# A third batch's front taken early: batch 2's first transposes, logits and projections run beside the first searches, every queue gets a new order, and the bias matmul contracts over 96 rows

## The chip, the core and the metric

One core of one Trainium2 chip runs the whole program. The metric is the device time of one execution in microseconds (us), here the median of three executions. TensorE is called PE (its weight loads PEld), VectorE DVE, ScalarE ACT, GpSimd POOL and SyncE SP. PE's clock is granted at one of two levels, 1.2 or 2.4 GHz; a profile writes them as 0.5 and 1.00.

## The reference, cut to what matters

```
x: (4, 512, 256)                       # 4 batches of 512 tokens, 16 row tiles of 128 tokens
xn = layernorm(x)
# layer 0, attention-like: cumulative sum over tokens
q, k, v = xn Wq + bq, xn Wk + bk, xn Wv + bv
context = (elu(q)+1) * cumsum((elu(k)+1) * v) / 4
# layer 0, genes
logits = (rms(xn) * norm_w) Wc^T / temperature        # (tokens, 512)
w = softmax(top 32 of 512 logits)                     # the "search": 4 rounds of 8 maxima
e = w @ genes[top];  ffn = tanh(e Wd^T) * rms(xn) * norm_w * (e Wu^T) * scale
x = x + context Wo^T + bo + ffn
xn = layernorm(x)
# layer 1: r = rms(xn); q,k,v = r w_qkv; gated cumulative sums -> y;
#   u, g = y w_swiglu;  out += (u * silu(g)) w_out
# layer 1: 16 experts, 2 per token, + a shared expert (352 hidden) on every token
```

## The kernel before, in words

All five engines get one long list of calls, written out by hand or by a planner; each call (a closure of `build`) waits on semaphores, issues its instructions and increments a semaphore. Nothing is reordered: an engine that waits in one call holds all calls behind it. So the order of the five lists is the schedule.

A batch b goes through a *front* (layer 0), a *middle* (layer 1's gated sums), and *shared chunks*; after all batches come the *expert tiles*.

- Front. DVE `stats1(b)` and `ratio1(b)` and ACT `lroot1(b)` make the layer norm's numbers, ACT `normal(b, i)` (L618) applies them to row tile i, PE `turn1(b, h)` (L299) transposes, ACT `xcopy1` (L622) copies out of PSUM into FE. PE `logits(b, i)` makes 128x512 logits in a PSUM bank, PE `kproj`, `vproj`, `qproj` (each with j = 0, 1) the projections, also in banks (all of these through `products`, L280). The operands are f32, and the profile shows each such product as two matmul records. DVE searches: `topa`, `topb`, `tope`, `topf`, `topg` (L954 to L978) per row tile; ACT `expert`, `unsel`, `total`, `emcopy` and POOL `topc` turn the result into weights; PE `emturn` (L328) and `express` apply them to the genes; PE `ffn` (L344, with 96 rows) and `oproj(b, j)` follow. `oproj` first writes the bias (L351: `w_one` times `bo_r`, 64 rows: a rounded part, a rest and zeros, in f32r), then eight matmul records of Wo on top (L355). DVE `joined` (L1001) ends the front.
- Middle. `stats2`, `lroot2`, `normal2`, `xroot`, PE `turn2`, `turnr`, `qproj2`, `kproj2`, `vproj2`, `meanq` (L395), `meank` (L400), `gates`; the operands are split in a rounded and a rest part (f32r), three matmuls for one product. DVE `qhat` (L1011), `khat` (L1018), `wsum`, `divisor`, `refine` and POOL `qfold`, `kfold`, `correct`, `quotient` belong to it.
- Shared chunks: for k = 0 to 10, PE `dgate(b, k)`, `dup(b, k)`, `ddown(b, k)` with ACT `dact`, `dround` and DVE `dtanh`, `dtimes` between them. They depend only on their own batch, and are strewn through the PE list as filler. Two buffers (HS, HQ) hold a chunk, so chunk k + 2 may begin when `ddown` of k is done.
- Expert tiles: 47, each PE `xturn(j)`, `xup(j)`, `hturn(j)`, `xdown(j)`, with two or three buffers for each step, and POOL fetching rows (`xfetch`) and scattering them (`yput`). The address of a tile's weights comes from registers that `locate` fills.

Banks 0 to 5 rotate; each call names its bank, and `take` waits for the last reader of it. Batch b uses the buffers FA to FG of b % 2, so batch 2's front can start only when batch 0 has left them: FA[0] is refilled by `fetch(2)` after `yspill(0)`, and FB to FE pass from batch 0's middle.

Where the PE list had nothing to do beside the first searches, `awake(n)` issues 2n matmul records on a constant tile `still` (L292); the list has 35 of them, 10 ahead of the first transpose, 15 up to the express of batch 0, 10 around the first `turn2`.

Weights that are split in two f32r parts come in pieces: SP `stagein(n)` loads piece n, ACT `prep(n)` (L587) makes the rounded part, POOL `prep(n)` (L1293) the rest. `PREP` lists them; `HIDDEN` and `DOWN` say how many must be ready for chunk k (nine for the gate and up products of k = 9 and 10, ten for ddown from k = 7 on). All nine are loaded in the first microseconds.

Of the kernel before, what the change touches and what calls it, by code (L numbers as in the profile page):

```python
# [8 lines left out]
F32R = mybir.dt.float32r  # L9
# [5 lines left out]
P = 128  # L15
# [15 lines left out]

TILES = 47
# [20 lines left out]
    "yh yl xh xl dg tg g2 du dh r0 rl rlp dw od "  # L53

# [29 lines left out]
def build(nc, x, vec, cst, wqkv0, wo0, wc, genes, wdu, wqkv1, wsg, wout, gate, sgu, sdn, gu, dn, part_d, out):  # L84
    with ExitStack() as ctx:
# [31 lines left out]
        w_one, bo_r = tile("w_one", P, F32R, 64), tile("bo_r", D, F32R, 64)  # L117
# [79 lines left out]
        d_xb, d_yb = sem("d_xb"), sem("d_yb")  # L197
# [3 lines left out]
        d_stage = [sem(f"d_stage{n}") for n in range(3)]  # L201
# [1371 lines left out]
```

## Time and profile before

| | us |
|---|---|
| median of 3 executions | 531.91 (530.75 to 852.44) |
| span of the profiled execution, first to last instruction | 529.7 |
| what the median has beyond that span | 2.2 |

The profiled execution has no time of its own beside its span; 531.91 - 529.7 = 2.2 us is taken as what lies around it. PE is busy in 507.5 us, DVE in 354.0, ACT in 296.0 and POOL in 272.7. "Busy" is the union of the records; a matmul record ends by a model about 0.17 us after its successor has begun, so the rate of PE is read from start to start.

### The profile page before, as it was taken

What the parts mean: (1) busy time and instruction counts of PE and PEld (TensorE: products, weight loads), DVE (VectorE), ACT (ScalarE), POOL (GpSimd) and SP (SyncE); (2) the same over time, 40 slices, a digit from 0 to 9 for tenths busy, and PEclk for the clock granted to TensorE, in tenths of its full rate; (3) what the DMA queues carried; (4) which work ended last, traced back from release to release, by engine and by line L of the source; (5) the groups of instructions that cost most, each with busy time, mean ns of one, the idle gap of its engine ahead of it and who ended that gap; (6) DMA issues with size and microseconds to landing.
All of it is one profiled execution on the core that took longest, in us unless ns stands there. A gap on an engine that the chain in (4) does not pass through costs nothing.

```text
span 529.7 us, 7444 instructions
## 1 busy us (share of the span) xinstructions
PE 507.5 (96%) x2488; PEld 384.8 (73%) x2488; DVE 354.0 (67%) x735; ACT 296.0 (56%) x577; POOL 272.7 (51%) x207
## 2 busy tenths in 40 slices
PE   7989999988999999999997999999999999999995
PEld 5565577766577766877885888887777777777684
DVE  4999995786998998847899895743232323323347
ACT  3788798785767758767653636225343343424321
POOL 0475648383472373383256346464576576666510
PEclk9999999998999999999999999999999999999999
DMA  8900031026020001037001850583322232223267
GB/s 271 372 6 1 1 124 37 0 100 220 1 80 40 1 1 41 1 129 243 1 1 44 292 179 14 187 232 98 108 91 89 71 100 83 97 80 89 71 242 265
DMA packets 19813, 54.32 MB, mean 103 GB/s; under 512 B 3312, under 2 KB 5792, under 8 KB 19776
## 3 DMA queue, kind: packets, MB, share of 16 engines
q1 hardware_dynamic: 15264, 41.52, 22.7%
q0 software_dynamic: 4512, 12.33, 7.7%
q8 instruction: 21, 0.34, 0.3%
q14 instruction: 16, 0.13, 0.1%
HBM read 36.14 MB, written 17.74 MB: 102 GB/s over the span
## 4 chain that ended last, share of the span: by engine, by line
PE 74%; DVE 15%; DMA 4%; issue 3%; ACT 2%; POOL 1%; SPq 1%; DVEq 0%; POOLq 0%; ACTq 0%
PE bank L280 52%; PE bank L442 9%; PE bank L355 3%; PE bank L474 2%; PE bank L501 2%; DMA fa<-in_x 2%; DMA ga<-y_rows 2%; DVE tk L972 1%; DVE m L970 1%; PE bank L328 1%; DVE fe L1029 1%; PE bank L400 1%; PE bank L292 1%; DVE tk L978 1%; DVE rw L1235 1%
## 5 line engine op out<-in xcount | busy, mean ns | idle before, releaser
L1214 DVE TENSOR_TENSOR m_h<-m_h,bank 128x176 f32<-128x176 f32 x47 | 15.8, 337 | 82.9 <-ACT m_h L789 82.9
L280 PE MATMUL bank<-mw,m_xt 128*128 x188 | 66.4, 476 | 0.2
L1362 POOL DMA_INDIRECT y_rows<-m_y,dest x47 | 46.9, 997 | 30.7 <-DVE m_y L1221 20.9
L1356 POOL DMA_INDIRECT xg<-xn_rows,tab x47 | 45.5, 969 | 28.0 <-PE bank L474 19.3
L280 PE MATMUL bank<-yhr,wsg_h 128*128 128x512 f32 x128 | 56.0, 437 | 0.8 <-ACT fc L721 0.8
L280 PE MATMUL bank<-hyr,wsg_h 128*128 128x512 f32 x128 | 50.1, 392 | 0.0
L280 PE MATMUL bank<-yhr,wsg_l 128*128 128x512 f32 x128 | 50.1, 391 | 0.0
L280 PE MATMUL bank<-mw,m_ht 88*128 x188 | 48.3, 379 | 0.0
L280 PE MATMUL bank<-fe,w_qkv 128*128 128x512 f32 x96 | 44.5, 594 | 0.6 <-ACT fe L622 0.6
L1347 POOL TENSOR_TENSOR hs0r<-hs,hq0r 128x512 fp32r<-128x512 f32 (+1 forms) x17 | 23.4, 1374 | 39.8 <-ACT hq0r L776 39.8
L280 PEld LDWEIGHTS bank<-mw,m_ht 88*128 88x128 f32 x188 | 35.2, 189 | 11.1 <-issue 0.4
L280 PEld LDWEIGHTS bank<-mw,m_xt 128*128 128x128 f32 x188 | 32.0, 189 | 14.9 <-issue 2.3
L789 ACT ACTIVATE m_h<-bank 128x176 f32<-128x176 f32 x47 | 14.9, 317 | 46.5 <-PE bank L280 46.5
L1098 DVE SCALAR_TENSOR_TENSOR hs<-hs,bank 128x512 f32<-128x512 f32 (+1 forms) x44 | 29.9, 680 | 14.7 <-PE bank L280 7.9
L1301 POOL TENSOR_TENSOR tk<-tk 128x512 f32<-128x512 f32 x16 | 21.3, 1334 | 27.9 <-ACT tk L680 27.8
L1347 POOL TENSOR_TENSOR hs1r<-hs,hq1r 128x512 fp32r<-128x512 f32 (+1 forms) x16 | 21.1, 1321 | 28.0 <-ACT hq1r L776 28.0
L782 ACT ACTIVATE m_xt<-bank 128x256 f32<-128x256 f32 x47 | 17.9, 381 | 29.9 <-PE bank L474 29.9
L572 ACT ACT_TABLE_LOAD x23 | 29.5, 1283 | 6.7 <-PE bank L442 5.6
L1088 DVE SCALAR_TENSOR_TENSOR hs<-hs,bank 128x512 f32<-128x512 f32 (+1 forms) x33 | 22.4, 680 | 15.4 <-ACT hs L771 15.4
L280 PEld LDWEIGHTS bank<-fe,w_qkv 128*128 128x128 f32 x96 | 17.5, 190 | 18.2 <-issue 16.3
L280 PE MATMUL bank<-w_wc,fe 128*128 128x512 f32 x64 | 29.9, 594 | 0.9 <-DVE w_wc L859 0.9
L280 PEld LDWEIGHTS bank<-yhr,wsg_h 128*128 128x128 f32 x128 | 24.1, 189 | 7.5 <-issue 1.7
(241 smaller groups left out, 1419.7 us busy)
## 6 DMA issues: line engine op xcount, KB each, us to landing
mw<-in_gu SPq DMA_DIRECT2D x16, 352.0 KB
ga<-y_rows SPq DMA_DIRECT2D x8, 512.0 KB, 8.1
mw<-in_dn SPq DMA_DIRECT2D x16, 176.0 KB
wsg_w<-in_wsg SPq DMA_DIRECT2D x4, 512.0 KB, 14.8
spilled_r<-fb SPq DMA_DIRECT2D x4, 512.0 KB, 2.8
spilled_x<-fa SPq DMA_DIRECT2D x4, 512.0 KB, 4.0
xn_rows<-fg SPq DMA_DIRECT2D x4, 512.0 KB, 3.6
hx<-spilled_x SPq DMA_DIRECT2D x4, 512.0 KB, 3.7
```

The costliest lines, as they stand in the source:

```text
L280: mm = e.matmul(o, a, b, start=n == 0, stop=n == len(terms) - 1)
L355: mm = e.matmul(o[:, i * D:(i + 1) * D], FF[b % 2][:, c, t:t + P], wov[:, c, :], start=False, stop=i + c == 2, skip_group_check=True)
L442: mm = e.matmul(o, a, w[0:m, r, :], start=k == 0 and i % 2 == 0 and z == 0, stop=False, skip_group_check=True)
L572: e.preload_act_table_set(name)
L782: e.activation(m_xt[j % 2][:, :], ps("jx", j)[:, 0:D], ACT.Copy).then_inc(s["jxc"], 1)
L1088: e.scalar_tensor_tensor(h, h, 1.0, ps("dg", b, k)[0:m, :], ALU.add, ALU.mult).then_inc(s["g2"], 1)
L1098: e.scalar_tensor_tensor(h[0:m, 1, :], h[0:m, 0, :], 1.0 if DIRECT[b] else 0.5, ps("du", b, k)[0:m, :], ALU.mult, ALU.mult).then_inc(s["dh ...
L1214: e.tensor_tensor(m_h[j % 3][:, :], m_h[j % 3][:, :], ps("ju", j)[:, 176:352], ALU.mult).then_inc(s["jh"], 1)
L1301: e.tensor_tensor(em, em, w, ALU.subtract).then_inc(s["tc"], 1)
L1347: e.tensor_tensor(HSr[c % 2][0:m, 0, :], HS[c % 2][0:m, 1, :], HQ[c % 2][0:m, 0, :].bitcast(F32), ALU.subtract).then_inc(s["rlp"], 1)
L1356: e.indirect_dma_start(out=xg[j % 3][:, :], out_offset=None, in_=xn_d, in_offset=bass.IndirectOffsetOnAxis(ap=tab[:, j:j + 1], axis=0)).th ...
L1362: e.indirect_dma_start(out=y_d, out_offset=bass.IndirectOffsetOnAxis(ap=dest[:, j:j + 1], axis=0), in_=m_y[j % 3][:, :], in_offset=None).t ...
```

## The change

Batch `EARLY` = 2 gets buffers of its own for the part of its front that has no search in it:

```diff
+        EA = also("early_x", stage_at, 1024)...          # its x, normalised x, transposed x:
+        ED = also("early_n", stage_at + 1024, 1024)...   # where HX, XH, HY are later
+        EE = big(also("early_t", stage_at + 2048, 1024))
+        EL = [also(f"early_l{n}", wsg_at + 4096 * n + 3072, 1024)... for n in range(2)]   # logits
+        EQ = {"q": big(also("early_q", stage_at + 8 * 1024, 1024)), "k": big(also("early_k", wout_at + 1024, 1024)), "v": ...}
```

New calls: SP `efetch` loads x[2] into EA (`fetch(2)` into FA[0] stays, for the residual sum). ACT `enormal(0..3)` writes ED, PE `eturn(0..1)` transposes it, ACT `excopy(0..1)` writes EE. PE `elogits(0..3)` and `eproject(0..5)` do for batch 2 what `logits(2, i)` and `kproj`, `vproj`, `qproj(2, j)` did, and ACT `elcopy(0..3)` and `epcopy(0..5)` carry the ten results from PSUM to EL and EQ:

```diff
+            def elogits(i, n):
+                q.wait_ge(s["wcf"], 2)
+                o = take(("el", i), n, s["ec"], i + 3)
+                q.wait_ge(s["ec"], i // 2 + 1)
+                products(o[:, :], [(EE[:, c, i * P:(i + 1) * P], wcv[:, c, :]) for c in range(2)]).then_inc(s["eg"], 1)
+            def elcopy(i):
+                q.wait_ge(s["eg"], i + 3)
+                e.activation(EL[i // 2][:, i % 2, :], ps("el", i)[:, :], ACT.Copy).then_inc(s["ec"], 1)
```

`topa(2, i)`, `expert(2, i)`, `phi(2, ...)` and `vtimes(2, j)` read EL and EQ in place of banks; `turn1(2)`, `xcopy1(2)`, `logits(2)` and the six projections of batch 2 are gone; `normal(2, i)` stays (FD is a factor of the ffn's product) and waits for `fetch(2)`. `stats1(2)` and `lroot1(2)` read EA and have small tiles of their own.

EL and EQ lie where the pieces 8 and 9 of the split weights go, so these are loaded late:

```diff
+                if n == 8:
+                    q.wait_ge(s["em"], 4 * EARLY + 4)
+                if n == 9:
+                    q.wait_ge(s["pv"], 2 * EARLY + 2)
-                e.dma_start(w[:, o:o + k], ap[:, o:o + k]).then_inc(d_stage[(n - 1) // 3], 16)
+                e.dma_start(w[:, o:o + k], ap[:, o:o + k]).then_inc(d_stage[STAGED[n]], 16)
...
+                else:                                    # xback(0); yback(0) waits for ec >= 12
+                    q.wait_ge(s["exn"], 4)
+                    q.wait_ge(s["eg"], 2)
```

The bias has 96 rows (64 before; the third block of 32 is zeros):

```diff
-        w_one, bo_r = tile("w_one", P, F32R, 64), tile("bo_r", D, F32R, 64)
+        w_one, bo_r = tile("w_one", P, F32R, 96), tile("bo_r", D, F32R, 96)
-    bo[0::32] = a["L0_attn_bo"]
+    bo[0:64:32] = a["L0_attn_bo"]
```

All five lists are new. Of the 35 `awake` the first 10 stay. The first third of the PE list, before and after:

```diff
-            awake(10); turn1(0, 0, 0); logits(0, 0, 1); turn1(0, 1, 2); logits(0, 1, 3); logits(0, 2, 4); kproj(0, 0, 5); kproj(0, 1, 0); vproj(0, 0, 2)
-            logits(0, 3, 1); vproj(0, 1, 5); turn1(1, 0, 0); awake(2); emturn(0, 0, 3); awake(2); express(0, 0, 3); qproj(0, 0, 4); awake(5); emturn(0, 1, 0); logits(1, 0, 1)
-            express(0, 1); emturn(0, 2, 0); awake(4); emturn(0, 3, 0); express(0, 2); awake(2); turn1(1, 1, 0); express(0, 3); logits(1, 1, 2); qproj(0, 1, 5)
-            kproj(1, 0, 1); kproj(1, 1, 0); ffn(0, 0, 4); vproj(1, 0, 5); ffn(0, 1, 3); ffn(0, 2, 1); logits(1, 2, 2); ffn(0, 3, 4); oproj(0, 0, 3)
...
+            awake(10); turn1(0, 0, 0); logits(0, 0, 1); turn1(0, 1, 0); logits(0, 1, 2); kproj(0, 0, 0); kproj(0, 1, 3); turn1(1, 0, 1)
+            logits(0, 2, 4); logits(0, 3, 1); qproj(0, 0, 0); emturn(0, 0, 3); vproj(0, 0, 2); vproj(0, 1, 3); express(0, 0, 5); eturn(0, 2)
+            eturn(1, 3); emturn(0, 1, 2); logits(1, 0, 3); express(0, 1); elogits(0, 4); elogits(1, 1); elogits(2, 4); elogits(3, 2)
+            logits(1, 1, 4); emturn(0, 2, 2); qproj(0, 1, 1); emturn(0, 3, 2); turn1(1, 1, 0); express(0, 2); express(0, 3); eproject(2, 0)
+            eproject(3, 2); eproject(4, 5); ffn(0, 0, 3); ffn(0, 1, 1); ffn(0, 2, 4); logits(1, 2, 0); ffn(0, 3, 5); kproj(1, 0, 2); kproj(1, 1, 3)
+            oproj(0, 0, 5); oproj(0, 1, 2); eproject(5, 4); vproj(1, 0, 3); vproj(1, 1, 0); logits(1, 3, 2); emturn(1, 0, 0); eproject(0, 3)
+            eproject(1, 5); turnr(0, 0, 4); turn2(0, 0, 1); turn2(0, 1, 0); express(1, 0, 3); emturn(1, 1, 5); turnr(0, 1, 1); qproj(1, 0, 0)
...
```

In the other lists: DVE makes `stats1(2)` and `ratio1(2)` between the searches of row tiles 1 and 2 of batch 0, and `topa(2, 0)`, `(2, 1)`, `(2, 2)`, `topb(2, 0)` and `tope(2, 0)` ahead of `joined(1, ...)`. ACT gets the new calls beside the first searches, and the preps 1 to 5 move back behind them. SP loads x[1] ahead of w_qkv0, and genes, wdu and wo0 behind the first three pieces. In the lists from batch 2's middle on, shared chunks come in pairs (`dgate` k and k + 1, `dup` k and k + 1, `ddown` k and k + 1), and expert steps in groups of two to five of one kind:

```diff
-            xturn(6, 4); hturn(4, 0); xup(5, 5); ddown(3, 1, 6, 7); xdown(3, 1); xturn(7, 3); hturn(5, 2); xup(6, 4); dgate(3, 3, 0); xdown(4, 5)
...
+            ddown(3, 0, 6, 7); hturn(3, 2); hturn(4, 3); hturn(5, 4); xdown(1, 5); xdown(2, 0); xdown(3, 2); xturn(9, 5); xturn(10, 3); xup(6, 0)
+            xup(7, 4); xup(8, 1); xdown(4, 0); ddown(3, 1, 6, 7); xturn(11, 3); xturn(12, 5); hturn(6, 2); hturn(7, 0); xup(9, 4); xup(10, 1)
```

## Rows read from the trace of the kernel before

**Rows 1.** The page, part 1: busy time of each engine.
```profile
PE 507.5 (96%) x2488; PEld 384.8 (73%) x2488; DVE 354.0 (67%) x735; ACT 296.0 (56%) x577; POOL 272.7 (51%) x207
```

**Rows 2.** Busy time of each engine in five stretches (start:end, length, then as headed).
```profile
core 0: us, PE busy (x) PEld busy (x) DVE busy (x) ACT busy (x) POOL busy (x), PEclk, DMA share, GB/s
...
20.00:97.40 77.40, 74.17 (x329) 49.93 (x328) 67.88 (x136) 66.92 (x121) 53.87 (x29) 1.00 0.16 60
...
97.40:241.80 144.40, 138.66 (x664) 101.62 (x664) 121.05 (x261) 101.45 (x184) 71.44 (x44) 0.98 0.18 63
...
241.80:300.00 58.20, 54.36 (x296) 45.29 (x295) 52.72 (x113) 34.49 (x55) 25.17 (x16) 1.00 0.26 88
...
357.00:501.00 144.00, 143.79 (x692) 108.53 (x690) 45.00 (x107) 54.35 (x157) 89.00 (x90) 1.00 0.29 90
501.00:529.70 28.70, 22.33 (x132) 19.33 (x130) 17.32 (x22) 5.36 (x10) 2.91 (x3) 1.00 0.66 238
```

**Rows 3.** Waits of PE: who was waited for, us, times, longest.
```profile
PE bank L280 <- DVE fd L1011: 3.1, 1, 3.1
```

**Rows 4.** The same busy times, of the instructions on the tile still alone.
```profile
20.00:45.00 25.00, 7.30 (x30) 5.39 (x30) 0.00 (x0) 1.00 0.25 101
...
60.00:80.00 20.00, 4.65 (x20) 3.64 (x20) 0.00 (x0) 1.00 0.24 91
```

**Rows 5.** Timeline of PE (start, us, what, count): batch 0's products, then batch 2's first and last.
```profile
15.38 5.31 PE L280 MATMUL bank<-fe,w_qkv 128*128 128x512 f32 x12
20.53 1.88 PE L280 MATMUL bank<-w_wc,fe 128*128 128x512 f32 x4
...
132.15 0.60 PE L299 MATMUL bank<-w_cst,fd 128*128 128x128 f32 x4
...
171.55 1.88 PE L280 MATMUL bank<-fe,w_qkv 128*128 128x512 f32 x4
```

**Rows 6.** Timeline of DVE: a batch's first statistics, and a search step.
```profile
13.51 1.41 DVE L876 BATCH_NORM_STATS2 bn<-fa 128x6 f32<-128x256 f32 x4 [0.24 <-DMA fa<-in_x]
...
15.25 0.67 DVE L954 MAX8 m<-bank 128x8 f32<-128x512 f32 x1
...
16.62 0.68 DVE L963 MAX8 m<-tk 128x8 f32<-128x512 f32 x1
```

**Rows 7.** Timeline of ACT: three passes over a row tile.
```profile
106.93 1.57 ACT L633 ACTIVATE fg<-fb,sm 128x256 f32<-128x256 f32 x3
```

**Rows 8.** The page, part 6: a transfer of 512 KB, issue to landing.
```profile
hx<-spilled_x SPq DMA_DIRECT2D x4, 512.0 KB, 3.7
```

**Rows 9.** Timeline of PE: a matmul with 96 rows, and two bias matmuls with 64.
```profile
90.02 0.40 PE L344 MATMUL bank<-wdu_r,fg1r 96*128 96x512 f32 x1
90.26 0.40 PE L280 MATMUL bank<-xhr,sgu_h 128*128 128x512 f32 x1
...
92.61 0.49 PE L351 MATMUL bank<-bo_r,w_one 64*128 64x512 f32 x1
93.03 1.99 PE L355 MATMUL bank<-w_wo,ff 128*128 128x256 f32 x8
94.95 0.50 PE L351 MATMUL bank<-bo_r,w_one 64*128 64x512 f32 x1
```

**Rows 10.** Timeline of PE: the beginnings of two expert tiles.
```profile
423.81 0.38 PE L474 MATMUL bank<-w_cst,xg 128*128 128x128 f32 x2
...
426.30 0.38 PE L474 MATMUL bank<-w_cst,xg 128*128 128x128 f32 x2
```

**Rows 11.** Busy times and granted clock again, and PE's timeline, where the clock fell.
```profile
114.00:118.00 4.00, 3.40 (x19) 2.87 (x20) 3.14 (x5) 3.35 (x5) 4.00 (x3) 0.88 0.34 131
...
115.53 2.07 PE L280 MATMUL bank<-w_gate,fa 128*128 128x16 f32 x16
...
118.44 0.63 PE L280 MATMUL bank<-ff1r,qkv_h 128*128 128x512 f32 x1
118.87 0.63 PE L280 MATMUL bank<-fe1r,qkv_h 128*128 128x512 f32 x1
```

More of the change, by code:

```diff
@@ L30 @@
 SPLIT = (True, True, True, False)
+EARLY = 2
 TILES = 47
@@ new lines, in tensor @@
+            dup(0, 0, 0); meank(0, 4); oproj(1, 0, 3); oproj(1, 1, 2); vproj2(0, 0, 1); vproj2(0, 1, 3); dgate(0, 1, 2); dup(0, 1, 5); dup(0, 2, 0)
+            turnr(1, 0, 4); turnr(1, 1, 1); ddown(0, 0, 6, 7); dgate(0, 2, 3); qproj2(1, 0, 4); qproj2(1, 1, 1); meanq(1, 5); kproj2(1, 0, 2)
+            kproj2(1, 1, 3); vproj2(1, 0, 4); turn2(1, 0, 1); turn2(1, 1, 0); meank(1, 5); vproj2(1, 1, 1); gates(1, 5); ddown(0, 1, 6, 7)
+            ddown(0, 2, 6, 7); dgate(0, 3, 3); dgate(0, 4, 2); emturn(2, 0, 5); dup(0, 3, 0); dup(0, 4, 1); dgate(0, 5, 4); dgate(0, 6, 3)
@@ new lines, in tensor @@
+            ddown(1, 0, 6, 7); ffn(3, 2, 5); dgate(1, 2, 0); ffn(3, 3, 3); meanq(2, 1); kproj2(2, 0, 5); dup(1, 2, 3); kproj2(2, 1, 1)
+            oproj(3, 0, 2); oproj(3, 1, 4); meank(2, 3); dup(1, 3, 2); dgate(1, 3, 3); vproj2(2, 0, 4); ddown(1, 1, 6, 7); dgate(1, 4, 1)
+            vproj2(2, 1, 5); turn2(3, 0, 4); turn2(3, 1, 0); ddown(1, 2, 6, 7); turnr(3, 0, 3); turnr(3, 1, 2); dup(1, 4, 5); dgate(1, 5, 1)
+            gates(3, 0); ddown(1, 3, 6, 7); ddown(1, 4, 6, 7); dgate(1, 6, 2); dup(1, 5, 3); dup(1, 6, 0); route1(3); qproj2(3, 0, 2)
@@ L1235, in combine @@
                 e.tensor_tensor(r, o, r, ALU.add).then_inc(s["cb"], 1)
-            statsh(); stats1(0); start(); ratio1(0); wcfold(); topa(0, 0); stats1(1); topa(0, 1); topb(0, 0); ratio1(1); tope(0, 0); topb(0, 1)
-            topf(0, 0); tope(0, 1); topg(0, 0); topa(0, 2); topf(0, 1); topb(0, 2); topg(0, 1); tope(0, 2); topa(0, 3); topf(0, 2); topb(0, 3)
-            topg(0, 2); tope(0, 3); topf(0, 3); topg(0, 3); topa(1, 0); wuscale(); topb(1, 0); kplus(0); tope(1, 0); vtimes(0, 0); vtimes(0, 1)
@@ new lines, in vector @@
+            topa(2, 3); dtanh(0, 5); dtimes(0, 5); topb(2, 3); kplus(2); tope(2, 3); stats1(3); topf(2, 3); topg(2, 3); dtanh(0, 6); ratio1(3)
+            dtimes(0, 6); dtanh(0, 7); vtimes(2, 0); vtimes(2, 1); kvsum(2, 0); kvsum(2, 1); dtimes(0, 7); topa(3, 0); topa(3, 1); qplus(2)
+            dtanh(0, 8); elow(2); dtimes(0, 8); rscale(2); uptimes(2, 0); uptimes(2, 1); topb(3, 0); topb(3, 1); uptimes(2, 2); uptimes(2, 3)
+            tope(3, 0); tope(3, 1); topf(3, 0); topg(3, 0); topf(3, 1); topg(3, 1); joined(2, 0); joined(2, 1); stats2(2); dtanh(0, 9); dtimes(0, 9)
```

469 lines of the change are left out of this document (262 added, 207 removed).

## The prediction

> **What bounds the kernel now.** Read the busy times of the whole span first: PE 507.5 of 529.7 us, DVE 354.0, ACT 296.0 [rows 1]. Then the stretches, cut at the end of a batch's front: 97.4 us is where batch 1's `joined` ends, 241.8 where batch 3's does [rows 2]. The reader is to see two things. PE is full nearly everywhere: idle 3.2 us in the first of these stretches (77.40 - 74.17), 5.7 in the second, 3.8 in the third, 0.2 in the expert stage, 6.4 in the last (which holds the final stores). And PE is not alone: DVE is busy in 67.9 of 77.4 us of the first stretch, in 121.1 of 144.4 of the second and in 52.7 of 58.2 of the third. The longest single wait of PE is 3.1 us for a middle's `qhat` [rows 3].
>
> So the time is PE's work plus PE's idle. A part of the "busy" is no work: after 20 us, 30 + 20 matmul records run on the constant tile [rows 4]. They were there because the searches of batch 0 and 1 (DVE) set the pace and PE had nothing else. That is the room that the change wants to fill.
>
> **Part 1: batch 2's early front.** Its PE cost is read from start to start: twelve records take 20.53 - 15.38 = 5.15 us, 0.429 each [rows 5]. Ten products (four logits, six projections) of four records make 40 x 0.429 = 17.2 us; eight transposes at 0.60 for four, ends overlapping, about 0.9. Sum 18.1 us. Before, all of it lies between 132.15 and 173.3 us [rows 5], in a stretch where PE hardly waits, so every microsecond of it is on the path. After, it lies ahead of 97 us. PE's work is the same in all: nothing is saved by moving it, except where it takes the place of idle time or of `still`.
>
> What goes: 50 `still` records. Their rate follows from 7.30 us for 30 and 4.65 for 20 with overlapping ends, at most 12.0 us; by 256 columns against 512 at 0.429, 0.215 each, 10.7. I take 10.7 (bounds 10.7 and 12.0).
>
> First stretch, to the end of batch 1's front: +18.1 - 10.7 = +7.4, less the bias (below) 1.6: PE would end it 5.8 later with idle unchanged. Do the others allow it? DVE gets `stats1(2)` and `ratio1(2)`, 15.25 - 13.51 = 1.74 and about 0.7, and of batch 2's search three first steps (16.62 - 15.25 = 1.37 each), a `topb` and a `tope` (0.6 and 0.7): 2.4 + 5.4 = 7.8 us [rows 6]. The 5.4 fall where DVE waits for batch 0's middle (its idle time in the stretch is 9.5 us [rows 2]). ACT gets four normalisations and ten copies out of PSUM that did not exist before, 14 x 0.52 = 7.3 us [rows 7], and some 2 us that only move, less two calls (1.3) that leave: 66.9 + 8 = 75 us. In a stretch of 77.4 + 5 = 82.4 that is 91%, against 86% before. It fits, narrowly. I take +5 for the stretch (bounds +1, if the idle is filled too, and +8).
>
> Second stretch, to the end of batch 3's front: 144.4 - 18.1 - 1.6 (bias) = 124.7 us with PE's idle unchanged. DVE's work falls by the 7.8 us done earlier, to 113.3: 91% of it, where it was 84%. Two full engines that feed each other lose something, so I add 2 us (bounds -3 and +10; the second is a rival below): 126.7. Sum so far: +5 - 17.7 = -12.7.
>
> The cover that I count on in this stretch: `meanq(1)` now stands straight behind `qproj2(1, 1)` and must wait for an ACT square and a POOL sum, about 2 us; `meank(1)` has a projection and two transposes more ahead of it and loses a wait of the same size. I set these against each other.
>
> **Part 2: late pieces.** `stagein(8)` waits until batch 2's last `expert` is done; SP holds `stagein(9)`, `rback(1)`, `yback(1)` and two stores behind it. A transfer of 512 KB lands in 3.7 us [rows 8]; between that `expert` and ACT's `prep(8)` stand a root with a table load, a `dact`, an `unsel` and two normalisations, more than 5 us of ACT, and the piece is first needed by chunk 9 of batch 0, later still. `yback(1)` serves batch 1's chunks, after chunk 10 of batch 0. Price nothing; if that cover were gone, one stall of some 4 us. The second load of x[2] is 0.5 MB where DMA is 16% busy [rows 2]: nothing. `xback(0)` and `yback(0)` wait for early work that ends long before.
>
> **Part 3: bias with 96 rows.** One half of `oproj` takes 94.95 - 92.61 = 2.34 us; its eight records of 256 columns are 8 x 0.215 = 1.72, so the 64-row bias matmul costs 0.62 where a 96-row matmul of the same 512 columns takes 90.26 - 90.02 = 0.24 [rows 9]. Gain 0.38 x 8 halves = 3.1 us, half of it before 97.4 and half in the second stretch. Bounds 0 and 3.1: I take the upper, since the 96-row neighbour is the same kind of instruction. The Trainium skill speaks against this edit: "TensorE: Matmul & The Clock Gate", section "Why this matters for your kernels", says that a single matmul with 32 rows takes the time of one with 128, that is, that rows don't enter. By it the edit would be worth nothing and the sum 3.1 us higher. The rows here show 0.62 against 0.24, though which of the two, rows or the change of array mode, they can't say.
>
> **Part 4: new orders.** From 241.8 on PE's work is the same (58.2 + 57 + 144 + 28.7). The third stretch has 3.8 us of idle, 3.1 of it that one wait; a new order may keep or lose it: -1. Expert tiles: two beginnings lie 426.30 - 423.81 = 2.49 us apart [rows 10], and all are at PE's rate with 0.2 us of idle in 144 [rows 2]. Grouping gives back at most what address registers cost between a short transpose and the `xup` behind it, some tenths of a us per tile; and it can add waits. I take -0.5 (bounds -4 and +11). Tail: the same amount of shared chunks behind the last expert: 0.
>
> **Sum.** 529.7 - 12.7 - 1 - 0.5 = 515.5 us of span, and 2.2 around it: 517.7, say 517.5. The same from the other side: 529.7 less 10.7 of `still` and 3.1 of bias is 515.9 if PE's idle time stays what it is. Against the median 531.91 that is -2.7%. A measurement of this kernel can tell about 2% from no change, that is 521.3 and 542.5.
>
> **The rivals.**
> 1. *The saved PE time turns into waits for DVE and ACT.* Before, DVE had 144.4 - 121.1 = 23.3 us of idle in the second stretch, waits in its chains. If it keeps all of them, the stretch is 113.3 + 23.3 = 136.6 instead of 126.7: +9.9, time 527.4. For: ACT and DVE are both above 90%. Against: part of that idle lay before 137 us, where DVE had no search yet; now it has batch 2's.
> 2. *Groups stall in the expert stage and the paired chunks.* With two buffers the third of three `xdown` in a row needs a copy made after the first; PE covers that with one `xdown` of 0.86 us against 0.38 of copy and its signals. If some 14 groups lose 0.8 us each: +11, time 528.5. Against: PE idles 0.2 us there now, and other work stands between most groups.
> 3. *The idle is filled as well.* First stretch +1 instead of +5, the third's wait gone, and registers hidden: -4 -2 -4, time 507.5.
> 4. *The clock falls, and the kernel is slower.* At 115.5 PE ran light `gates` matmuls after a wait, the granted clock of the 4 us is 0.88, and then the same matmul takes 118.87 - 118.44 = 0.43 us instead of 0.23 [rows 11]: the lower level. Up to 97.4 us the clock is 1.00 throughout [rows 2], with the `still` records in. If their absence let it fall from 24 to 60 us, about 34 us of PE work would take 68: 517.5 + 26 after what idle absorbs, 543.5. It decides from 14 us of early work at the lower level. Against: their place is taken by real products. The Trainium skill, "TensorE: Matmul & The Clock Gate", section on PE-mode transpose, says that transposes don't count as PE being busy; eight of the new records are such, and by it this rival would be a little likelier. No row here tells transposes apart.
>
> **How the numbers follow.** Forecast 0.56 (511 to 523), rival 1 0.17, rival 2 0.10, rival 3 0.12, rival 4 0.05. The range takes in rivals 1 and 3 and leaves out about 2 in 10: 507 to 528. Faster by over 2%: rival 3 (0.12), nine tenths of the forecast (0.50), the better end of rival 1 (0.04): 0.66. Slower by over 2%: most of rival 4, 0.04. Within 2%: 0.30.
>
> **What would show it.** Right: `still` records only before 8 us; 40 f32 products of batch 2 between 27 and 72 us; `joined(1)` ending at 99 to 105, `joined(3)` at 226 to 232; bias to next record 0.24 us; no clock below 1.00 before 97 us. Wrong: `joined(3)` after 235 with PE idle over 10 us ahead of it (rival 1), the expert stage longer than 146 us (rival 2), a half-speed stretch early (rival 4), or a stall of ACT at `prep(8)`.

## The result: slower by 5%, and the profile after

The changed kernel takes 557.10 us in the median of four executions (555.72 to 558.78) against 531.33 before; the ratio is 1.050 with the interval 1.047 to 1.054. Forecast were 517.5 us, in a range from 507 to 528. The profiled execution has a span of 553.9 us, 24.2 more than before. Ratios, here and below, compare fast executions alone, that is, those within 1.5% of the fastest one of their kernel; the trace of e11 is of an execution outside that, so only its first 238 us are read.

The page of the changed kernel, part 1 (busy time of each engine):

```profile
PE 503.4 (91%) x2438; PEld 379.4 (68%) x2438; DVE 382.4 (69%) x735; ACT 298.8 (54%) x589; POOL 279.4 (50%) x207
```

Against [rows 1], PE's busy time fell by 4.1 us. DVE's rose by 28.4 us, with the same 735 instructions. That is the first thing to see: DVE was given nothing more to do.

Where the 24 us lie is read by cutting both spans where DVE begins the second half of the last `joined` of batch 1 and of batch 3. (The prediction took 97.4 us for the end of that half, but it is its start, and 241.8 is the end; by starts it is 97.4 and 241.2.) Busy times of the kernel before, cut so:

```profile
20.00:97.40 77.40, 74.17 (x329) 49.93 (x328) 67.88 (x136) 66.92 (x121) 53.87 (x29) 1.00 0.16 60
97.40:241.20 143.80, 138.06 (x662) 101.11 (x661) 120.45 (x261) 101.45 (x184) 71.44 (x44) 0.98 0.17 61
241.20:529.70 288.50, 278.07 (x1450) 223.49 (x1448) 154.04 (x297) 118.06 (x255) 147.03 (x130) 1.00 0.37 120
```

The changed kernel, cut at its own `joined` (107.7 and 249.0), and its late part once more at the first and last expert tile's copy:

```profile
20.00:107.70 87.70, 81.15 (x325) 50.29 (x324) 79.59 (x157) 72.72 (x135) 50.59 (x27) 0.98 0.11 39
107.70:249.00 141.30, 125.89 (x630) 97.07 (x630) 130.85 (x255) 100.29 (x180) 81.36 (x47) 0.96 0.19 64
249.00:361.30 112.30, 99.86 (x536) 83.02 (x535) 92.24 (x145) 51.42 (x80) 49.71 (x33) 0.95 0.37 119
361.30:517.00 155.70, 149.10 (x733) 113.22 (x732) 45.40 (x107) 54.31 (x156) 91.53 (x92) 1.00 0.34 101
517.00:553.90 36.90, 29.55 (x166) 24.93 (x164) 20.59 (x28) 8.27 (x18) 5.82 (x6) 0.97 0.52 193
```

Three differences: the first stretch is 10.3 us longer (107.7 - 97.4; forecast +5), the second 2.5 shorter (forecast -17.7), the rest 16.4 longer (304.9 - 288.5; forecast -1.5). Two traces of one and the same front order can differ by 2 us: in e8 below, whose front is that of the kernel before, the second stretch took 141.9 us instead of 143.8. In the second stretch PE now idles 15.4 us (5.7 before), and DVE is busy 130.9 us of 141.3, although it was to have 7.8 us less work than before.

The longest waits of PE in the changed kernel (waited for, us, times, longest), where [rows 3] had a single one of 3.1 us:

```profile
PE bank L437 <- DVE r_pos L1238: 4.5, 1, 4.5
PE bank L303 <- DVE hs L1173: 4.4, 3, 2.2
PE bank L370 <- DVE fb L1012: 4.0, 1, 4.0
PE bank L500 <- DVE r_at L1278: 3.6, 4, 2.3
PE bank L370 <- DVE g_s L1145: 3.3, 1, 3.3
PE bank L484 <- DVE hs0r L1188: 3.1, 1, 3.1
```

All are waits for DVE. Take the third: PE stands from 69.8 to 73.8 us for `vtimes(1, 1)`. DVE's timeline ahead of it, and POOL's (start, us, what):

```profile
66.59 0.38 DVE L950 BATCH_NORM_AGGREGATE mv<-bn 128x2 f32<-128x6 f32 x4
66.88 3.30 DVE L1002 SCALAR_TENSOR_TENSOR fb<-fb,fc 128x1024 f32<-128x1024 f32 x1
70.10 2.30 DVE L956 SCALAR_TENSOR_TENSOR sm<-mv,sm 128x8 f32<-128x8 f32 x1
72.32 1.40 DVE L1012 SCALAR_TENSOR_TENSOR fb<-bank,w_vec,fb 128x512 f32<-128x512 f32 x2
```

```profile
65.67 3.43 POOL L1379 TENSOR_TENSOR qkv_l<-qkv_w,qkv_h 128x1536 fp32r<-128x1536 f32 x1
69.06 4.27 POOL L1379 TENSOR_TENSOR sgu_l<-sgu_w,sgu_h 128x1024 fp32r<-128x1024 f32 x2
```

An operation on 8 columns took 2.30 us, and one on 1024 columns 3.30. The reader is to see the ends: 66.88 + 3.30 = 70.18 is the end of POOL's first subtraction (69.10) plus some 1.1 us of the instruction's own; 70.10 + 2.30 = 72.40 is the end of the first of POOL's pair (its own record ends at 72.38). By these ends DVE stood still until POOL was done. Groups of equal form show how much and for whom. Before (count, busy, mean ns):

```profile
L1029 DVE TENSOR_TENSOR_SCAN fe<-fg 128x512 f32<-128x512 f32 x8 | 9.7, 1213 | 0.2 <-PE bank L280 0.2
L1188 DVE TENSOR_TENSOR r_bt<-w_cst,slot_f 128x512 fp32r<-128x512 f32 x8 | 5.4, 680 | 0.0
L886 DVE SCALAR_TENSOR_TENSOR sm<-mv,sm 128x8 f32<-128x8 f32 x4 | 0.6, 154 | 0.0
L970 DVE MAX8 m<-tk 128x8 f32<-128x512 f32 x32 | 21.9, 686 | 0.3
```

After:

```profile
L1114 DVE TENSOR_TENSOR_SCAN fe<-fg 128x512 f32<-128x512 f32 x8 | 15.5, 1965 | 0.0
L1273 DVE TENSOR_TENSOR r_bt<-w_cst,slot_f 128x512 fp32r<-128x512 f32 x8 | 9.8, 1230 | 0.0
L956 DVE SCALAR_TENSOR_TENSOR sm<-mv,sm 128x8 f32<-128x8 f32 x4 | 3.8, 953 | 0.8 <-ACT sm L651 0.8
L1055 DVE MAX8 m<-tk 128x8 f32<-128x512 f32 x32 | 22.0, 686 | 0.4
```

MAX8, with one operand, has the same mean as before, 686 ns; scans and other forms with two operands in SBUF do not. Every DVE instruction of both traces was sorted so (match-value loads left out): does it have two operands in SBUF (or is it a copy or tensor-scalar within SBUF), did it begin while a tensor instruction of POOL still had 0.1 us or more to run, and did it last over 0.15 us longer than the shortest of its form? Of 71 that are of these kinds and began beside POOL, 65 were longer; of 233 of these kinds that did not begin so, 3; of 344 of other kinds that began beside POOL, none. The sum of the delays is about 24 us before and 50 after; in the second stretch it is 5.9 and 21.4. So the kernel before already contained such waits, and the prediction read them as DVE's work.

The Trainium skill states a rule for this in "SBUF — State Buffer", section "Who interferes with whom": VectorE's second pair of ports is GpSimd's only one; a VectorE instruction with two SBUF inputs contends with a GpSimd instruction that reads SBUF, and one in a two-port mode contends with GpSimd; whichever issues first has the pair for its whole instruction. The trace agrees: 65 of 71. This section of the Trainium skill bore on the change, and the prediction did not weigh it.

### The profile page after: what moved, and what is told of

Read it like the earlier page. It is cut to its first block, busy times and chain, and to the rows that moved or that the text cites. A ratio compares the mean times of both kernels' runs of the same rounds, so it can differ in the third digit from the quotient of the medians.

```text
span 553.9 us, 7351 instructions
## 1 busy us (share of the span) xinstructions
PE 503.4 (91%) x2438; PEld 379.4 (68%) x2438; DVE 382.4 (69%) x735; ACT 298.8 (54%) x589; POOL 279.4 (50%) x207
## 4 chain that ended last, share of the span: by engine, by line
PE 39%; DVE 31%; issue 8%; DMA 7%; POOL 7%; ACT 6%; DVEq 0%; SPq 0%; ACTq 0%; POOLq 0%
PE bank L303 27%; PE bank L484 5%; DMA y_rows<-m_y,dest 4%; POOL xg L1443 3%; DMA xg<-xn_rows,tab 3%; DVE fe L1114 2%; DVE r_at L1278 2%; POOL y_rows L1449 2%; DVE hs L1183 2%; DVE fa L1121 2%; DVE tk L1057 1%; DVE m L1055 1%; DVE hs L1173 1%; PE bank L516 1%; PE bank L397 1%
## 5 line engine op out<-in xcount | busy, mean ns | idle before, releaser
L303 PE MATMUL bank<-mw,m_xt 128*128 x188 | 61.6, 465 | 4.6 <-DVE m_y L1306 2.7
L303 PE MATMUL bank<-yhr,wsg_h 128*128 128x512 f32 x128 | 54.2, 423 | 2.9 <-DVE hs L1173 2.1
L1306 DVE TENSOR_SCALAR m_y<-bank,gslot 128x256 f32<-128x256 f32 x47 | 22.2, 482 | 45.0 <-DMA y_rows<-m_y,dest 27.2
L1387 POOL TENSOR_TENSOR tk<-tk 128x512 f32<-128x512 f32 x16 | 24.0, 1515 | 56.6 <-ACT tk L748 56.6
L303 PE MATMUL bank<-mw,m_ht 88*128 x188 | 45.3, 383 | 0.0
L1183 DVE SCALAR_TENSOR_TENSOR hs<-hs,bank 128x512 f32<-128x512 f32 (+1 forms) x44 | 29.7, 683 | 18.4 <-ACT hs L836 12.4
L1434 POOL TENSOR_TENSOR hs0r<-hs,hq0r 128x512 fp32r<-128x512 f32 (+1 forms) x17 | 26.0, 1530 | 27.1 <-ACT hq0r L844 26.9
L303 PEld LDWEIGHTS bank<-mw,m_ht 88*128 88x128 f32 x188 | 33.2, 189 | 6.0 <-issue 1.9
L839 ACT ACTIVATE hs<-bank 128x512 f32<-128x512 f32 (+1 forms) x33 | 19.2, 594 | 29.0 <-PE bank L484 17.3
L303 PE MATMUL bank<-fe,w_qkv 128*128 128x512 f32 x72 | 32.6, 594 | 0.0
L863 ACT ACTIVATE m_ht<-bank 88x256 f32<-88x256 f32 x47 | 17.1, 378 | 25.9 <-PE bank L303 17.8
```

The costliest lines, as they stand in the source:

```text
L303: mm = e.matmul(o, a, b, start=n == 0, stop=n == len(terms) - 1)
L839: e.activation(HS[c % 2][0:m, 0, :], ps("dg", b, k)[0:m, :], ACT.Tanh, scale=0.5).then_inc(s["tg"], 1)
L1183: e.scalar_tensor_tensor(h[0:m, 1, :], h[0:m, 0, :], 1.0 if DIRECT[b] else 0.5, ps("du", b, k)[0:m, :], ALU.mult, ALU.mult).then_inc(s["dh ...
L1306: e.tensor_scalar(m_y[j % 3][:, :], ps("jd", j)[:, 0:D], gslot[:, j:j + 1], None, ALU.mult).then_inc(s["jy"], 1)
L1387: e.tensor_tensor(em, em, w, ALU.subtract).then_inc(s["tc"], 1)
L1434: e.tensor_tensor(HSr[c % 2][0:m, 0, :], HS[c % 2][0:m, 1, :], HQ[c % 2][0:m, 0, :].bitcast(F32), ALU.subtract).then_inc(s["rlp"], 1)
```

## The experiments

Below, "joined(1)" and "joined(3)" are the starts of the last `joined` of batch 1 and 3 in the profile: 97.4 and 241.2 before, 107.7 and 249.0 in the changed kernel. Ratios are to the kernel before. "After" is the changed kernel.

**e1: the bias alone.** The kernel before with

```diff
-        w_one, bo_r = tile("w_one", P, F32R, 64), tile("bo_r", D, F32R, 64)
+        w_one, bo_r = tile("w_one", P, F32R, 96), tile("bo_r", D, F32R, 96)
```

> The kernel before with the bias of 96 rows alone. The step of the prediction: eight halves of oproj shorter by 0.38 us each on PE, so up to 3.1 us less, if PE's time there is on the path (ratio 0.994). Theory 'DVE sets the pace in the second stretch': only part of it comes through, 0 to 2 us. Either way the bias record to the next takes 0.24 us.

Measured: 528.05 us beside 529.18 of before on the same chip, ratio 0.9991 (0.9970 to 1.0012). The timeline of PE at the place of [rows 9]:

```profile
91.68 0.80 PE L351 MATMUL bank<-bo_r,w_one 96*128 96x512 f32 x1
92.32 1.89 PE L355 MATMUL bank<-w_wo,ff 128*128 128x256 f32 x8
93.86 0.58 PE L351 MATMUL bank<-bo_r,w_one 96*128 96x512 f32 x1
94.28 1.46 PE L355 MATMUL bank<-w_wo,ff 128*128 128x256 f32 x6
```

From one bias to the next it is 93.86 - 91.68 = 2.18 us, where [rows 9] have 2.34. The second bias still holds PE for 94.28 - 93.86 = 0.42 us, as before. Two other steps got shorter, by the starts of the single records: the one to the bias from the record before it (0.31 us before, 0.03 now), and the one from the first Wo record to the second (0.32 before, 0.22 now). Together that is 0.38 us, as forecast; from the record ahead of the bias to the second Wo record it is 0.37 to 0.39 us in six of the eight halves, and 0.19 and 0.23 in the two where PE waited ahead of the bias. So PE was given back 2.7 us, but the interval of the ratio leaves at most 1.6 us of time. The size was right; that all of it is on the path was not.

**e2 and e3: POOL writes without reading.** In the kernel before (e2) and after (e3), POOL's subtractions that make low parts become memsets:

```diff
-                e.tensor_tensor(HYr[:, j, :], HY[:, j, :], YH[:, j, :].bitcast(F32), ALU.subtract).then_inc(s["yl"], 1)
+                e.memset(HYr[:, j, :].bitcast(F32), 0.0).then_inc(s["yl"], 1)
```

and the same in `xlow`, `dlow` and `prep`. The low parts are then zero, so the products lack their small terms.

> The kernel before; POOL's 79 subtractions that make the low parts (dlow, ylow, xlow, prep) are memsets of the same tiles, so the low parts are zero: POOL writes and reads nothing of SBUF there, and takes less time. Theory 'port' (a DVE instruction with two SBUF operands, or a copy or tensor-scalar within SBUF, waits for the POOL instruction that is under way): 24 us of DVE's time in the kernel before are such waits, about half of them at these POOL instructions, and some 3 to 10 us of them are on the path. Theory 'order' (the new order itself costs the time): 0 to 3 us here.

> The changed kernel with the same edit as e2. Theory 'port': the extra DVE time (382 us busy against 354) goes, DVE's busy time falls below 360, no instruction on DVE outlasts its usual time at a memset, and the kernel gains 15 to 30 us, clearly more than the kernel before gains by the same edit. Theory 'order': it gains no more than the kernel before does by the same edit (0 to 5 us), and the gap of 5% stays.

(The traces show 59 such subtractions on POOL, not 79.)

Measured: e2 525.32 us, ratio 0.993 (0.990 to 0.996), 3.9 us less than before. e3 534.22 us, ratio 1.011 (1.007 to 1.015); after, by its ratio of 1.050, would be 555.8 beside the same 529.2, so the edit gave 21.5 us. joined(1) came at 101.8 us and joined(3) at 233.3: the second stretch took 131.5 us. The same DVE instructions as above, beside POOL's memsets, in e3:

```profile
66.64 1.19 DVE L1002 SCALAR_TENSOR_TENSOR fb<-fb,fc 128x1024 f32<-128x1024 f32 x1
67.75 0.16 DVE L956 SCALAR_TENSOR_TENSOR sm<-mv,sm 128x8 f32<-128x8 f32 x1
```

```profile
65.41 1.38 POOL L1379 MEMSET qkv_l<- 128x1536 f32 x1
66.72 1.32 POOL L1379 MEMSET sgu_l<- 128x1024 f32 x2
```

1.19 instead of 3.30, 0.16 instead of 2.30, though POOL was at work at both starts (66.64 lies in the first memset, 67.75 in the second one of the next row's pair). Of 22 DVE instructions with two SBUF operands that began inside a memset in e2 and e3, 21 took their usual time. So it is POOL's reading that blocks. The same section of the Trainium skill says so too: only a GpSimd instruction that reads SBUF contends with two SBUF inputs. DVE was busy 356.1 us in e3 and 341.8 in e2; the difference is again delays, at POOL's other reads (26.5 us in e3, 11.0 in e2). The memsets are shorter too (0.53 us for 512 columns against 1.29), so not all of the 21.5 us need be the port; but the same saving of POOL time in e2 gave 3.9, and e12 below takes most of the delays away with POOL's work unchanged.

**e4: does the clock pay?** In after, seven calls of

```diff
+            def hold(n, k):      # k matmuls of 256 columns on constants, into bank n, which is free
...
+                for _ in range(k):
+                    e.matmul(banks.t[n][:, 0:D], ident, w_cst[:, C_ID:C_ID + D], start=True, stop=True)
```

> The changed kernel; ahead of seven calls at which PE waits 1.9 to 4.2 us, 3 to 8 matmuls of 256 columns on constants (0.43 us each) run into a free bank, and fit into the wait. Theory 'clock' (PE's waits make the clock fall for 3.4 us each after them, 24 us at the lower level in all): four of the seven spells of low clock go, each worth 1.7 us of PE work, so 4 to 7 us less. Theory 'DVE sets the pace': the clock stays up in those places and the time moves by less than 2 us.

Measured: 554.52 us, ratio 1.049 (1.046 to 1.052): 1.3 us less than after, within the error. Busy times and granted clock of after around the wait at 69.8, and the same in e4:

```profile
69.00:73.00 4.00, 0.78 (x2) 0.00 (x0) 4.00 (x4) 0.56 (x2) 4.00 (x3) 1.00 0.00 0
73.00:78.00 5.00, 4.22 (x9) 2.30 (x10) 4.96 (x6) 5.00 (x13) 3.01 (x3) 0.66 0.00 0
```

```profile
69.00:73.00 4.00, 4.00 (x18) 3.05 (x17) 4.00 (x3) 0.18 (x1) 4.00 (x3) 1.00 0.00 0
73.00:78.00 5.00, 4.44 (x15) 2.16 (x14) 5.00 (x5) 5.00 (x12) 3.01 (x3) 1.00 0.00 0
```

The clock of the stretch behind the wait is 1.00 instead of 0.66 (1.2 GHz for a part of it), as the clock theory expected, and the mean over the span rose from 0.976 to 0.985. In all, three spells at the lower level went and a new one came, so 28.2 us of them became 19.0, less than was meant. DVE is busy for nearly all of both stretches, and the time hardly moved. At the most the 9.2 us could have given back 4.6. The low clock doesn't explain the loss of 26 us.

**e6 and e10: only the early front.** The order of after up to 107.8 us, then the kernel before's order; in e6 SP kept its changed list, in e10 SP too went back:

```diff
-            fetch(2); rback(0); yspill(1); fetch(3); rspill(1); stagein(8); stagein(9); rback(1); yback(1); ...
+            rspill(1); fetch(2); yback(0); ...; yspill(1); fetch(3); stagein(8); stagein(9); rback(1); yback(1); ...
```

> The changed kernel's order up to 107.8 us (batch 2's early front and all), then on every engine the order of the kernel before for the calls that are left; the last two pieces come in where batch 2's projections are used up. Theory 'DVE sets the pace between 100 and 250 us': the 18 us of PE work that went early don't shorten the stretch; joined(3) comes at 250 to 257 us and the kernel takes 540 to 556 us. The prediction's theory (PE sets the pace): joined(3) at 230 to 236, 520 us.

> As e6, and SP's list in the order of the kernel before as well, with the two late pieces behind the load of x[3]. Between batch 1's joined and batch 3's the PE has 112 us of work (131.6 before). Theory 'DVE sets the pace there': joined(3) stays at 250 to 255 us, and the late stages then run as before: 540 to 550 us. The prediction's theory, PE sets the pace: joined(3) at 230 to 236 us.

Measured: e6 555.60 us, ratio 1.048 (1.045 to 1.052); e10 544.42 us, ratio 1.027 (1.023 to 1.030). joined(3) at 253.5 and 253.6 us, in e10 144.0 us behind joined(1), where the kernel before needs 143.8 with batch 2's 18 us of PE work still in it. The stretch did not get shorter by taking PE work out of it. That PE alone sets its pace was wrong. Not all of this is a chain of DVE's own: DVE's delays beside POOL rose from 5.9 to 9.6 us there, and the granted clock was 0.93 instead of 0.98; neither was tested apart in this order.

**e7, e9 and e8: the late orders.** e7: the order of after up to 249.1 us, then that of before, but SP's list as changed; e9: SP's list as before too from there. e8: the kernel before up to 241.8 us, then the changed order. At batch 3's `meanq`, PE's list of e9 (-) and of e8 and after (+):

```diff
-            ddown(1, 5, 6, 7); ddown(1, 6, 6, 7); meanq(3, 0); dgate(1, 8, 0); dup(1, 8, 1)
+            dgate(1, 8, 4); ddown(1, 5, 6, 7); ddown(1, 6, 6, 7); meanq(3, 3); dup(1, 8, 3)
```

> The changed kernel's order up to 249.1 us (batch 3's joined), then the order of the kernel before on every engine. PE loses 35 us after that point in the changed kernel, 13.5 in the kernel before. Theory 'the new late orders (groups, pairs, and what DVE and POOL do at once) cost it': the time falls by 8 to 20 us, to 536 to 548. Theory 'the late loss comes from what the front left behind': less than 4 us.

> As e7, and SP's list too in the order of the kernel before from 249.1 us on (in e7 SP kept the changed order, and an xup waited 5.1 us for a load of expert weights). Theory 'the new late orders, the order of the loads among them, cost it': time 536 to 546 us, the expert stage loses 6 to 8 us instead of 14. Theory 'the late loss comes from the front': as e7, 550 us.

> The kernel before up to 241.8 us, then the changed kernel's order on every engine (without the early front, with all pieces loaded at the start, 64 rows). Theory 'the new late orders cost it': 540 to 552 us, 10 to 22 more than before, with DVE waits at POOL instructions risen from 24 us to over 32. Theory 'the late loss comes from the front': within 4 us of before.

Measured: e7 552.24 us, 1.043 (1.037 to 1.049); e9 541.73 us, 1.021 (1.018 to 1.024); e8 558.51 us, 1.056 (1.052 to 1.059). e7 was a mismatch of my own: the expert weights came in the changed order and were used in the old one, which its waits of PE show:

```profile
PE bank L303 <- issue: 5.1, 1, 5.1
```

With e9 it is clean: from joined(3) to the end 539.6 - 249.2 = 290.4 us, against 304.9 in after, and 288.5 before. So 14 to 15 us of the 26 are the new late order. e8 says the same from the other side: put behind the old front it costs 28 us. That is above the 10 to 22 expected, and DVE's delays rose only to 27.1 us, not over 32: in the part behind joined(3) by 3.0 us (16.3 to 19.3), where the time rose by 27. So the delays by themselves do not account for what the late order costs. Both e8 and after have a wait of 4.5 us for the same chain. DVE's routing ahead of PE's `meanq(3)` in after, and POOL meanwhile:

```profile
275.91 2.37 DVE L1225 TENSOR_SCALAR e_u<-r_inc 128x16 uint32<-128x16 f32 x1
278.31 1.21 DVE L1227 TENSOR_SCALAR e_u<-e_u 128x16 uint32<-128x16 uint32 x1
279.55 1.21 DVE L1229 CAST e_n<-e_u 128x16 f32<-128x16 uint32 x1
280.80 1.24 DVE L1231 TENSOR_TENSOR_SCAN e_n<-e_n 128x16 f32<-128x16 f32 x1
282.07 2.30 DVE L1233 TENSOR_TENSOR e_n<-e_n 128x16 f32<-128x16 f32 x1
284.30 2.62 DVE L1234 TENSOR_TENSOR r_bas<-r_inc,r_cnt 128x256 f32<-128x256 f32 x1
```

```profile
275.84 2.40 POOL L1421 TENSOR_TENSOR fa<-fa,fd 128x1024 f32<-128x1024 f32 x1 [7.96 <-ACT fd L814]
278.20 1.29 POOL L1434 TENSOR_TENSOR hs0r<-hs,hq0r 128x512 fp32r<-128x512 f32 x1
279.44 1.30 POOL L1434 TENSOR_TENSOR hs1r<-hs,hq1r 128x512 fp32r<-128x512 f32 x1
280.69 1.30 POOL L1408 TENSOR_TENSOR fc<-fc 128x512 f32<-128x512 f32 x1
281.93 2.41 POOL L1399 TENSOR_TENSOR fb<-fb,fg 128x1024 f32<-128x1024 f32 x1
```

Each tiny DVE operation ends where a POOL instruction ends: this chain on 16 columns ran at POOL's pace, each link, released by the one before it, starting a little behind POOL's next. Until its `r_pos` is written, `route1` holds bank 3, and `meanq(3, 3)` takes that bank. In the kernel before `meanq(3)` takes bank 0, and the first seven links of the chain took 2.8 us (273.28 to 276.09). The 3.1 us of [rows 3] are a wait behind a later part of the same routing, two casts and conversions of 2.32 and 2.21 us beside POOL; e2 took them to 0.9.

**e11: two lists alone.** The changed kernel, with the lists of PE, ACT and SP untouched; 64 of 433 DVE calls and 24 of 199 POOL calls stand more than two places elsewhere, such as

```diff
-            upnorm(1); prep(6); prep(7); dlow(0, 0); correct(0); quotient(0); ...; dlow(0, 4); topc(2, 2)
+            upnorm(1); prep(6); dlow(0, 0); correct(0); quotient(0); ...; dlow(0, 4); prep(7); topc(2, 2)
-            dlow(1, 6); qfold(3); residual(3); correct(2); xlow(2, 0); kfold(3)
+            dlow(1, 6); quotient(2); qfold(3); correct(2); kfold(3)
```

> The changed kernel with the lists of PE, ACT and SP untouched and the calls of DVE and POOL put in another order, so that fewer DVE instructions with two SBUF operands begin while POOL is at work and the calls that PE waits for come first. Theory 'port and the order of these two engines': DVE's waits for POOL fall from 50 us to 20 to 30, and the time by 14 to 26 us (530 to 542). Theory 'the early front and PE's order themselves cost it': less than 6 us.

Measured: ratio 1.024 (1.017 to 1.031), 543 us beside 530.7: about 14 us less than after, at the lower end of what was expected. In the trace, DVE's delays beside POOL fell from 50 to 23 us, and joined(3) came at 237.7.

**e12, e13 and e14: is the early front worth anything?** e12 is e9 with DVE and POOL reordered in the manner of e11 (54 and 30 calls by more than two places); e13 the kernel before with 96 rows, `routeb` in two calls and such a reordering of its own (some 33 and 21 calls); e14 is e12 with `hold` ahead of five calls:

```diff
-            upnorm(1); prep(6); prep(7); dlow(0, 0); correct(0); quotient(0); qfold(1); residual(1); kfold(1)      # e12
+            upnorm(1); dlow(0, 0); prep(6); correct(0); quotient(0); qfold(1); kfold(1); residual(1); prep(7)
...
+            def routec():                                                                                        # e13
...
-            meanq(1, 5); ... ddown(0, 1, 6, 7); ... ddown(0, 2, 6, 7); ... dgate(1, 3, 5); ... ddown(3, 9, 6, 7)
+            hold(2, 4); meanq(1, 5); ... hold(0, 6); ddown(0, 1, 6, 7); ... hold(0, 4); ddown(0, 2, 6, 7); ... hold(0, 7); dgate(1, 3, 5); ... hold(0, 5); ddown(3, 9, 6, 7)
```

> The kernel of e9 (changed front, the old order from 249.1 us on) with DVE and POOL calls reordered in the same manner. Theory 'port and order': 522 to 532 us, so the early front is worth at most some 8 us against the kernel before; joined(3) at 236 to 242 us (249 without). Theory 'the early front costs time itself': above 536 us.

> The kernel before with 96 rows for the bias, the second part of routeb as a call of its own, and the calls of DVE and POOL reordered in the same manner; no early front, old PE, ACT and SP lists. If order and port are what counts, this is the fastest: 518 to 525 us, and e12 no faster than it. If the early front has a value of its own once DVE is free, e12 is the faster of the two.

> The kernel of e12 (early front, old late order, DVE and POOL reordered) with 4 to 7 matmuls on constants ahead of five calls at which PE waits 2.0 to 3.3 us. e12 has 24 us of low clock, 17 of them between 119 and 143 us, right behind such waits. Theory 'clock': these spells go, and each gives back up to 1.7 us: 524 to 528 us, the fastest kernel here. Theory 'DVE's chain sets the pace there': as e12 within 1.5 us, as in e4.

Measured: e12 531.22 us, ratio 1.0016 (0.9997 to 1.0035); e13 531.44 us, 1.0028 (1.0007 to 1.0050); e14 528.05 us, 0.9951 (0.9930 to 0.9972). joined(3) in e12 came at 236.6, as expected, and the time was in the range given. Against e9, which differs only in the order of DVE's and POOL's calls, DVE's delays fell from 44.7 to 13.1 us and the time by some 10 (1.021 to 1.002), with no work taken away: this is the plainest evidence that the delays cost time. e13 missed its expectation of 518 to 525. It doesn't show that fewer delays are worth nothing with the old front, since its reordering hardly removed any (22.3 us left of 24). e14 is, by the ratios, the fastest version that computes the whole result, 0.5% below before and 5% below after. The stretch where it differs from e12, first e12 and then e14:

```profile
119.00:143.00 24.00, 19.45 (x82) 15.71 (x81) 21.42 (x35) 14.61 (x23) 14.26 (x9) 0.72 0.48 168
```

```profile
119.00:143.00 24.00, 22.17 (x117) 18.03 (x118) 21.81 (x36) 15.41 (x24) 14.31 (x9) 1.00 0.47 170
```

Here the clock does pay, 3.2 us in all: joined(3) comes 2.7 us earlier. Low clock fell from 23.9 to 2.6 us, by 21.3. Per us of low clock taken away that is 0.15 us of time, and in e4 it was 0.14 (1.3 of 9.2), where half a us each would come back if PE set the pace throughout. Of PE's speed little reached the end in either; with e4's uncertainty of some 2 us the two can't be told apart.

**e16: the port's share in the front.** e9 with the memsets of e2.

> The kernel of e9 (changed front, old late order, 541.7 us) with POOL's low-part subtractions as memsets, as in e2 and e3. In e3 the edit gave 21.5 us, in e2 3.9. Theory 'the front's share of the port waits is what the early front costs': 12 to 18 us less than e9, 524 to 530 us. Theory 'the port costs mostly in the late stages, with their new order': 4 to 8 us less, as with the old order throughout (e2).

Measured: 523.18 us, ratio 0.984 (0.979 to 0.988): 18.5 us less than e9, 20 by the ratios. Its stretches, as above (cut at 102.1 and 233.7):

```profile
20.00:102.10 82.10, 79.54 (x325) 49.48 (x324) 74.10 (x156) 72.48 (x135) 39.97 (x27) 1.00 0.11 40
102.10:233.70 131.60, 123.03 (x630) 95.59 (x630) 120.17 (x255) 100.21 (x180) 59.34 (x47) 0.97 0.23 82
```

The first stretch ends 4.7 us later than before, and the second is 12.2 shorter, 131.6. By the ratios, e16 is 4.8 us below e2, by the spans of the two traces 1.9: with most of POOL's low-part reads out of the way the early front with the old late order does pay, by 2 to 5 us.

## Why the prediction was wrong

Forecast were 14 us less, measured are 26 more. By the ratios, of the 26: 15 of late order (after against e9); 16 of DVE's waits for POOL, mostly in the fronts (the memsets give 20 on e9 and 3.9 on the kernel before; what POOL's shorter time has of this is not measured apart); and -5 for what the early front yields (e16 against e2). These differences form a closed chain of runs, so that they add up is no test of them. The stretches of the traces, and DVE's delays beside POOL in each (sorted as above), in us:

| run | to joined(1) | second stretch | rest | delays in the three |
|---|---|---|---|---|
| before | 97.4 | 143.8 | 288.5 | 1.8, 5.9, 16.3 |
| after | 107.7 | 141.3 | 304.9 | 7.7, 21.4, 21.1 |
| e8 (old front, new late order) | 96.9 | 141.9 | 315.8 | 1.8, 6.0, 19.3 |
| e9 (new front, old late order) | 107.8 | 141.4 | 290.4 | 7.7, 21.4, 15.6 |
| e12 (e9, two lists reordered) | 102.3 | 134.3 | 293.4 | 2.1, 4.8, 6.2 |
| e2 (before, memsets) | 96.4 | 140.8 | 286.2 | 1.4, 1.9, 7.7 |
| e16 (e9, memsets) | 102.1 | 131.6 | 287.9 | 2.1, 10.5, 5.6 |
| e3 (after, memsets) | 101.8 | 131.5 | 297.7 | 2.1, 10.5, 13.9 |

The reader is to see two things. In the fronts fewer delays came with less time (e9 against e12 and e16), though not in proportion. In the late part the time goes with them only in part: the new late order costs 14.5 us with POOL's low-part reads (after against e9) and still 9.8 without them (e3 against e16, with 8.3 us more of delay at POOL's other reads), and 27 behind the old front with 3.0 us more of delay (e8). Which of its waits make up the rest stays open.

- **"DVE's work falls by the 7.8 us done earlier, to 113.3."** This is the step that failed. DVE's busy time in the second stretch rose to 130.9 us. The 120.5 of before had 5.9 us of waits for POOL in it, after has 21.4: 120.5 - 7.8 + 15.5 is 128.2, most of the way. I summed DVE and POOL as if they were independent. In e3 and e16, with POOL's low-part reads gone, the same lists gave joined(1) at 101.8 and 102.1 (forecast 102.4) and a second stretch of 131.5 and 131.6 (forecast 126.7).
- **"Before, PE hardly waits there, so every microsecond of it is on the path."** Wrong. A full PE showed that the old order fitted, with shared chunks as filler, and not that PE alone set the pace. e10 took 18 us of work out of PE's second stretch and it stayed at 144.0 us. With POOL's low-part reads gone, 9 of the 18 did come back (140.8 in e2, 131.6 in e16).
- **"+5 for the first stretch"**: +10.3; 5.9 of the difference went in e3. The place was the wait at 69.8 us, for two DVE instructions behind POOL's preps, which had been moved there from beside the first searches.
- **Part 2, late pieces**: nothing, as forecast. No wait for a stage piece shows in PE's list of after.
- **Part 3, the bias**: 0.37 to 0.39 us a half on PE where nothing else was waited for, as priced, but at most 1.6 us of time where 3.1 was. That this PE time is on the path was the wrong half of the term. The Trainium skill's statement that a matmul of 32 rows takes the time of one of 128 ("TensorE: Matmul & The Clock Gate", section "Why this matters for your kernels") does not carry over to the steps around a 64-row matmul here, 0.38 us longer in sum than around one of 96; the sum would have been nearer with it all the same.
- **Part 4, "-0.5" and "-1", bounds -4 and +11**: measured +14 to +16, and +28 behind the old front. This is the second step that failed, and as large as the first. The order was priced by the idle that the old one had left, and not by the waits that the new one makes; in the chain at 276 us they are DVE's for POOL (4.5 us of PE's time), the rest is open.
- **The rivals.** Rival 1 had the right mechanism and place (DVE's waits kept while PE's work goes) and priced 9.9; in the second stretch it was 14.6 (141.3 against 126.7). What it missed is that the waits for POOL would grow, where it only kept DVE's idle time. Rival 2 had the right place with the smaller part of the loss: in the expert stage of after PE idles 6.6 us of 155.7, 0.2 of 144 before; the stage is also longer because more work of the shared chunks stands in it (208 such matmul records, 137 before). Rival 4, a clock that falls for lack of `still`: no low clock before 73 us, so removing the 50 records did no harm by itself up to there; the clock fell behind the new waits, and taking a third of that away gave little (e4).

The `still` records did go (20 are left of 70), and the forecast counted their 10.7 us in full. In e16 against e2, the best case for them, 2 to 5 us show.

Not settled: how much of the late order's 14 to 15 us (28 behind the old front) is grouping, pairing, the choice of banks or the loads' order; no run changes one of these alone. Whether some order avoids the port waits altogether is open too: e12 has 13.1 us of them left.

## What to carry to other kernels

Ask of a "busy" engine whether its instructions are as long as their form is elsewhere: one line of groups by form, with its mean, tells work from waiting inside an instruction (here 1213 against 1965 ns for the same scan), and an order that moves VectorE work beside GpSimd work must be priced with it. A full engine shows that an order fits, not that this engine sets the pace; that is tested by taking some of its work out of the stretch. In a kernel whose order is written out by hand, a part that is moved and a list that is rewritten are two changes, to be measured apart.

## What was not expected of the hardware

- A chain of seven dependent VectorE instructions, five on 16 columns (0.17 to 0.19 us each when alone) and two on 256 (0.41 to 0.43), took 12.4 us in after (275.91 to 288.35) beside an unbroken row of GpSimd tensor instructions, 1.2 to 2.6 us each.
- GpSimd paid too, but less: of 42 of its tensor instructions that began inside such a VectorE instruction in after, 21 were longer, 14.7 us in all (before: 15 of 26, 6.3 us).
- A memset on GpSimd did not lengthen the VectorE instructions with two SBUF operands that began beside it (21 of 22, in e2 and e3).
- A 64-row matmul between matmuls of 128 rows cost 0.38 us more than one of 96 rows (e1): 0.28 us in the step ahead of it and 0.10 in the step after the next record, at equal 0.42 us in between.
